# VectorE's attention program: from a loop over samples to straight code with constant waits

## The reference, cut to what matters

```
x = _ln(src) * (1.0 + scale) + shift
q, k, v = x @ Wq + bq, x @ Wk + bk, x @ Wv + bv           # 16 heads of 16
scores = einsum(q / sqrt(16), k) + attention_bias         # 8 x 16 x 512 x 512
probs  = softmax(where(src_mask, -inf, scores))
x = x + (einsum(probs, v) @ Wo + bo)
h = _ln(x) * g2 + beta2
x = x + _gelu2(h @ W1 + b1) @ W2 + b2                     # 256 -> 1024 -> 256
```

## Time and profile before

| | |
|---|---|
| median of 3 runs | 1180.36 us (1176.86 to 1182.26) |
| profiled execution | 1177.85 us, of which span 1176.0 us |
| TensorE busy | 1032.5 us (88%) |
| VectorE busy | 819.4 us (70%) |
| ScalarE busy | 781.0 us (66%) |
| mean granted TensorE clock | 0.961 |

### The profile page before, as it was taken

How to read it: one execution, slowest core, us unless ns; L and a number is a source line. 1 busy time by engine, 2 the same in 40 slices (tenths; PEclk the granted TensorE clock), 3 DMA queues, 4 the chain that set the end, 5 groups by cost and what they waited for, 6 DMA issues and landing times. The chain is left out here.

```text
span 1176.0 us, 21651 instructions
## 1 busy us (share of the span) xinstructions
PE 1032.5 (88%) x6042; PEld 669.3 (57%) x6128; DVE 819.4 (70%) x2056; ACT 781.0 (66%) x1238; POOL 349.4 (30%) x464
## 2 busy tenths in 40 slices
PE   2599999989989989999998999994799998998863
PEld 2456556546555645655665656552677776776641
DVE  5586786766667758668686667774546788987665
ACT  2387787867768768777787778783456655756442
POOL 0205115112311311511321231003454456644421
PEclk9799999989999999999999999998799999999976
DMA  6777967966975887797697597833111101101001
GB/s 231 251 279 261 354 249 249 366 241 204 338 286 206 300 299 256 263 339 270 223 341 278 195 342 268 314 122 111 37 36 37 37 21 51 54 18 37 18 19 36
DMA packets 131304, 230.36 MB, mean 196 GB/s; under 512 B 8992, under 2 KB 58016, under 8 KB 127136
## 3 DMA queue, kind: packets, MB, share of 16 engines
q1 hardware_dynamic: 131232, 229.59, 55.2%
HBM read 187.62 MB, written 41.94 MB: 195 GB/s over the span
## 5 line engine op out<-in xcount | busy, mean ns | idle before, releaser
L682 DVE CUSTOM_DVE_ANT_0 prob<-s_bank,big 128x512 f32<-128x512 f32 x512 | 345.7, 687 | 165.1 <-PE s_bank L541 125.0
L827 ACT ACTIVATE prob<-prob,nmax 128x512 f32<-128x512 f32 x512 | 363.1, 723 | 71.6 <-DVE nmax L682 67.3
L550 PEld LDWEIGHTS t_bank<-ident,prob 128*128 128x128 f32 x2048 | 239.2, 141 | 206.4 <-issue 75.8
L550 PE MATMUL t_bank<-ident,prob 128*128 128x128 f32 x2048 | 319.2, 279 | 8.3 <-DVE pt L691 4.4
L834 ACT COPY pt<-t_bank 128x512 f32<-128x512 f32 x320 | 184.6, 577 | 90.0 <-PE t_bank L550 87.5
L540 PE MATMUL s_bank<-stack_k,stack_q 128*128 128x512 bf16 x426 | 163.2, 383 | 21.4 <-DVE nmax L682 21.4
L541 PE MATMUL s_bank<-mterm_early,ident_bf 128*128 128x512 bf16 x448 | 170.9, 381 | 6.4 <-issue 2.3
L691 DVE COPY pt<-t_bank 128x512 f32<-128x512 f32 x192 | 132.0, 687 | 38.8 <-PE t_bank L550 38.8
L563 PE MATMUL o_bank<-pt,val 128*32 128x512 f32 x1024 | 138.0, 614 | 0.7 <-ACT pt L834 0.7
L1631 POOL TENSOR_TENSOR gl<-big,gh 128x512 fp32r<-128x512 f32 x64 | 87.1, 1371 | 86.4 <-DVE gh L1336 86.4
L946 POOL TENSOR_SCALAR val<-vst 128x64 f32<-128x64 f32 x128 | 27.0, 245 | 278.5 <-PE o_bank L563 243.6
(11 more groups left out here) (176 smaller groups left out, 1623.0 us busy)
## 6 DMA issues: line engine op xcount, KB each, us to landing
big<-in_fside_Bx16xSxS SPq DMA_DIRECT2D x128, 1024.0 KB, 6.0
pieces_dram<-pieces SPq DMA_DIRECT2D x64, 384.0 KB, 7.8
stack_q<-pieces_dram SPq DMA_DIRECT2D x16, 1024.0 KB, 7.2
stack_k<-pieces_dram SPq DMA_DIRECT2D x16, 1024.0 KB, 8.7
pieces_dram<-pieces SPq DMA_DIRECT2D x32, 256.0 KB, 7.6
xin<-in_x SPq DMA_DIRECT2D x8, 512.0 KB, 6.5
x_dram<-x SPq DMA_DIRECT2D x8, 512.0 KB, 2.7
big<-x_dram SPq DMA_DIRECT2D x8, 512.0 KB, 3.5
```

Of the source, the lines that this page charges most:

```text
L550: last = pe.transpose(t_bank[n % 2][:, c * P:(c + 1) * P], prob[:, n % NT, c * P:(c + 1) * P], ident[:])
L682: dve.tensor_tensor_reduce(out=prob[:, n % NT, :], in0=s_bank[n % 3][:, :], in1=bias[:, h % NB, t, :], scale=-1.0, scalar=3e38, op0=ALU.ad ...
L827: act.activation(tile, tile, ACT.Exp, bias=nmax[:, n % NT:n % NT + 1], scale=-1.0).then_inc(exped.sem, 1)
```

## The change

VectorE's loop over the samples 1 to 6 becomes a Python loop: the same body is written out six times, with b a constant. Every wait of VectorE's attention program is then on a constant, and no register is computed. The calls of `apart` are gone from VectorE's program in all eight samples, and with them the semaphore. The helper `link`, which makes VectorE wait for an instruction of its own, no longer needs the sample. The other four engines are unchanged and keep their loops; so does VectorE's program of the network part.

```diff
@@ @block.vector
             links = [0]
-            per_link = 2 + NG
-
-            def link(b, ins):
+
+            def link(ins):

                 links[0] += 1
                 ins.then_inc(dve_link, 1)
-                dve.wait_ge(dve_link, links[0] if isinstance(b, int) else (b - 1) * per_link + links[0])
+                dve.wait_ge(dve_link, links[0])

@@ add_bias
                 dve.wait_ge(scored.sem, scored.at(b, n + 1))
                 dve.wait_ge(turned.sem, turned.at(b, n + 1 - NT))
-                apart(dve, dve_apart)
                 dve.tensor_tensor_reduce(out=prob[:, n % NT, :], in0=s_bank[n % 3][:, :],

@@ statistics
-                link(b, last)
-                apart(dve, dve_apart)
+                link(last)
...
@@ the samples
             for n in range(2):
                 add_bias(0, n)
             iteration(0, first=True)
-            before = links[0]
-            with dve.Fori(1, B - 1) as b:
+            for b in range(1, B - 1):
                 iteration(b)
-            assert links[0] - before == per_link
-            links[0] = before + (B - 2) * per_link
             iteration(B - 1, last=True)
```

More of the change, by code:

```diff
@@ L342, in attention_block @@
         pool_link = sem("pool_link")
-        dve_apart = sem("dve_apart")
         pool_apart = sem("pool_apart")
@@ L705, in normalise @@
                 dve.wait_ge(std_done.sem, std_done.at(b, 1))
-                link(b, dve.reciprocal(rstd[:], std[:]))
+                link(dve.reciprocal(rstd[:], std[:]))
                 for t in range(QT):
@@ L738, in spare_use @@
                     o = s[:, :].rearrange("p (t j e) -> p t j e", t=QT, j=G)
-                    link(b, dve.reciprocal(rsum[:], o[:, :, :, HD:HD + 1]))
+                    link(dve.reciprocal(rsum[:], o[:, :, :, HD:HD + 1]))
                     dve.tensor_tensor(con[:, :, i * G * HD:(i + 1) * G * HD].rearrange("p t (j e) -> p t j e", j=G),
@@ L776, in cut @@
                 high, mid, low = (pieces[:, u % 2, i, :] for i in range(3))
-                link(-1, dve.tensor_copy(high, proj[:, u % 2]))
-                link(-1, dve.tensor_tensor(rest[:], proj[:, u % 2], high, ALU.subtract))
-                link(-1, dve.tensor_copy(mid, rest[:]))
+                link(dve.tensor_copy(high, proj[:, u % 2]))
+                link(dve.tensor_tensor(rest[:], proj[:, u % 2], high, ALU.subtract))
+                link(dve.tensor_copy(mid, rest[:]))
                 dve.tensor_tensor(low, rest[:], mid, ALU.subtract).then_inc(cut_done.sem, 1)
```

## The result

The changed kernel takes 1148.53 us, the median of four runs (1147.64 to 1148.76), against 1178.91 us (1176.86 to 1182.26) of the kernel before in as many: a ratio of 0.9726 with the interval 0.9703 to 0.9749 (the ratio goes by all the runs; the two medians alone would give 0.9742). It is 2.7% faster where 2.0% were forecast, and the median lies at the very end of the range, which began at 1148. The profiled execution took 1147.64 us and its span 1145.8 us. The direction and the mechanism of the main term were right; one term of the sum, step 4, was much too small.

A forecast was written before the change was run, and what follows sets the result against it. TensorE, busy 88% of the span, was taken as the bound, VectorE counting only where TensorE waits. 1177.85 - 21.6 - 1 = 1155.3 us, plus half of 2.5 for the median, gave 1156.5 us; range 1148 to 1169 us.

The forecast's parts named there:

- step 4: VectorE without `apart`, wait on the bias instruction: starts some 0.1 us earlier, 1 us taken, between 0 and 9.6 us.
- Step 1: VectorE's five jumps back go, so samples 2 to 6 run like sample 1: 21.6 us less.
- samples alike: Sign for the jumps' term: samples 2 to 6 at 92 us each.
- TensorE's 3.36 us gone: Sign for the jumps' term: TensorE's wait of 3.4 us for VectorE at each seam disappears.
- no low clock near 239 and 338 us: Sign for the jumps' term: TensorE's lower granted clock behind the first two stalls, 4.1 us together, disappears.
- Step 2: Other engines keep their jumps, at most 0.3 us each and hidden: 0 taken, 1.5 us if uncovered.
- rival that gives half back: At the seams something else ends last, such as the bias transfer or another engine's jump: 1169 us, chance 0.10.
- Step 3: VectorE's 102 register instructions a sample go, about 25 us over the loop, hidden except where VectorE has been waiting.
- more is gained: Earlier VectorE starts let TensorE work without a wait in all eight samples, 8 us more: 1148 us, chance 0.08.
- Step 5: VectorE's program grows from 1034 to 2286 instructions; fetching in line costs between 0 and 18 us, 0 taken.
- slower rival: Fetching VectorE's program in line is exposed inside each sample: 1191 to 1261 us, chance 0.03.
- Step 6: Sample 7 and the network part keep their code but for the `apart` calls, entered without a jump before: 0.

The follow-up runs named there:

- e15: Kernel before, loops and `apart` kept, with 63 idle semaphore counts added to VectorE's sample 0, so its loop begins 63 instructions later: 1155.24 us, 0.9786.
- e3: Changed kernel with a tiny VectorE loop, run twice, at each of the five seams between samples 1 to 6: 1150.61 us, 0.9761.
- e4: Changed kernel with ScalarE's loop body lengthened from 246 to 374 instructions by two idle semaphore counts a step: 1195.04 us, 1.0138.
- e5: Changed kernel with ScalarE's loop body lengthened from 246 to 310 instructions by one idle semaphore count a step: 1190.87 us, a single run.
- e12: e5 with 64 more idle counts in sample 0, so ScalarE's body of 310 begins 64 instructions later: 1149.42 us, a single run.
- e7: Changed kernel with ScalarE's loop over samples 1 to 6 written out too: 1147.47 us, 0.9721.
- e1: Changed kernel with VectorE's `apart` instructions kept, waits still on constants and no VectorE loop over the samples: 1155.14 us, 0.9803.
- e6: Changed kernel with TensorE's loop over samples 1 to 6 written out too, its waits on constants: 1150.38 us, 0.9746.
- e9: Changed kernel with only VectorE's samples 1 to 3 written out, samples 4 to 6 a loop with `apart` and register waits as before: 1161.07 us, 0.9839.

## Why the prediction was too high

*Step 1, the five jumps (21.6 us): right.* The profile has 21.9 us, and e15 reaches 23.4 us in the medians by moving the loop alone. Taking sample 1 as the model was sound, and so was the forecast of each sign: samples alike, TensorE's 3.36 us gone, no low clock near 239 and 338 us. What I had as the reason, a jump whose target is no longer held, is what e3, e4, e5, e12 and e15 show. What they add is that it hangs on where the body begins. The 68 ns of the jump's own record were called in agreement with a figure of 108; they are about two thirds of it, and neither has a part in the 21.6.

*The rule on the store of instructions.* The Trainium skill, page Runtime: NRT & Kernel Launch, section Instruction fetch mechanics, gives most engines 512 instructions and has a taken branch fetch when its target is outside the window. By the 512 alone, bodies of 310 and 374 would jump freely; both stalled, and I should not have called the 374 an agreement. What the runs bear out is the part on the window; a body was held here where it can lie in three pieces of 128, and dropped where it touches four.

*Step 2, what is late next (0): right.* TensorE's and ScalarE's jumps are still there, and e7 gains nothing by taking one away. The rival that gives half back (1169) fell with samples 2 to 6 at 91.2 us under a DMA share of up to 0.83.

*Step 3, the registers (0): right in size, and not for the reason given.* Sample by sample e1 (no registers) lies 0.1 us below e15 (registers, no stalls), 91.94 against 92.02, and the medians are the same. I had put a register instruction between the wait for scores and the start. In the trace of before it runs ahead of the wait: at the place of sample 1 shown above the last one is done at 145.05 us, and both waits, for scores and for the transpose, stand on the `apart` instruction at 146.77. The order listing ahead of the prediction has that wait at a register row; the trace decides.

*Step 4, `apart` and the place of the wait (1 us): this step failed.* It is the term of the sum that was mis-sized: 6.6 us in the medians (e1 to after). In the profile 6 x 0.84 = 5.0 lie in samples 1 to 6 and some 1.2 in sample 0; the rest of the 8.3 is no larger than the scatter between executions. Two things went into it. The start came 0.18 us earlier, not 0.1: before, 0.18 us pass from the start of the 50 ns instruction with the waits (146.77) to the bias instruction (146.95). And I let argue the value down: there TensorE waits for VectorE only 1.2 us in sample 1, and I took this for what there is to gain. The same waits of TensorE, 1.2 us in all, are still there after, so they are not what shrank. These are its weight loads before in sample 1:

```profile
PEld s_bank L540 <- DVE nmax L682: 2.1, 6, 0.8
...
PEld t_bank L550 <- ACT pt L834: 4.2, 7, 0.8
...
PEld t_bank L550 <- DVE pt L691: 2.5, 5, 1.2
```

and after:

```profile
PEld s_bank L539 <- DVE nmax L679: 1.7, 5, 0.6
...
PEld t_bank L549 <- ACT pt L827: 3.7, 7, 0.8
...
PEld t_bank L549 <- DVE pt L688: 2.2, 5, 1.3
```

Each is 0.3 to 0.5 us shorter, and among them the wait for ScalarE's copy, which comes behind VectorE's bias instruction in the chain. TensorE's idle time shows little of it either. The windows seem to say 92.1 - 90.15 = 1.95 us before and 91.2 - 90.06 = 1.14 us after, but some 10 of the 603 matmul records of sample 1 are missing before (x593 in the earlier trace rows), and their time counts as idle. e15, the same loop with all its records, has 92.0 - 90.64 = 1.36 us. So only 0.2 of the 0.8 us lie in idle time, and the other 0.6 in busy time (90.64 against 90.06) for the same work; the ends of matmuls are modelled, so a held-up TensorE can look busy here.

The upper bound of 9.6 us held the result by luck: it was eight times the 1.2 us that did not change. The rival "more is gained" (1148 us) names the cause that acted, the earlier starts, and took 8 us for it with a chance of 0.08. The evidence against it was TensorE's share of 98%, and by sample 1 it left 1.36 to 1.95 us a sample, or 11 to 16 us over eight: room for the 6.6. That the rival's time was met to 0.5 us is in part luck, since executions of before scatter by several us.

*Step 5, the longer program (0): right.* In line a fetch costs nothing that shows: samples 1 to 6 of after are equal, at 91.21 us with 11 packets arriving in samples 2 to 6. The slower rival fell for VectorE; for TensorE's larger program e6 leaves up to 0.25 us a sample open.

*Step 6 (0): not told apart.* Sample 7 has the same waits as step 4 and should gain by them, but the 0.9 us by which sample 7 and the network differ is less than the 2.7 us by which they scatter between kernels.

With 6.6 us in step 4 in place of 1, the sum of the profiled execution's time would have been 1177.85 - 21.6 - 6.6 = 1149.7 us; the profiled execution of after took 1147.64 and the median is 1148.53. The reserve of 1.2 us for the median against the profiled execution was about what came: 0.9.

## What to carry to other kernels

Look at the time from each taken jump to the next instruction of that sequencer: where it is microseconds in place of 0.3, the loop's head has been dropped, and moving the loop by some tens of idle instructions, or shortening the body, may give back as much as writing it out. How many are needed can be counted: where the instruction packets arrive in the records gives the borders, and the body should touch one piece fewer. Where an engine waits for a result in a tight chain, name that wait first, so that it stands on the instruction itself, and put no counting instruction between. If a bound engine is 98% busy, the wait rows of its matmuls are no bound on what a shorter hand-over gives: here they stood still at 1.2 us while the sample lost 0.84. Measure one sample with the hand-over changed, and compare windows only where as many records stand in both.

## What the runs showed of the hardware

- A taken jump of the loops over samples cost 0.2 to 0.3 us or 4.7 to 6.4 us, with nothing between. Which of the two hung on body and place together: 246 free, 310 at one place dear and 64 instructions on free, 374 at one place dear and 57 or 63 on free. In all eight cases on VectorE and ScalarE a body in three pieces of 128 was free and one in four was dear.
- A held loop fetched nothing: no instruction packet in samples 2 to 6 of e15, 25 before.
- Idle semaphore instructions in a busy engine's queue were free: 128 a sample on ScalarE left the sample at 91.20 us.
- The place of a wait set the start behind a matmul's (modelled) end: 0.22, 0.18, 0.15 or 0.04 us.
- The lower clock behind a stall of TensorE is not certain: of before's five stalls two had it, of e9's two both, of e5's and e4's all five, in e4 for some 10 us each. That leaves room for what e4 cost beyond its stalls. It may also be why the runs of the kernel before scatter: beside e1 they reach from 1172.76 us at a mean granted clock of 0.967 to 1185.69 us at 0.955, but no experiment tested it.
